# Cross attention of a decoder layer: five steps of the score loop take other places

## The chip, the cores and the metric

One core of a Trainium2 chip runs the kernel. The metric is the device time of one launch in microseconds (us); lower is better. TensorE appears as PE (its weight loads as PEld), VectorE as DVE, ScalarE as ACT, GpSimd as POOL, SyncE as SP.

## What is computed

A decoder layer on x of 8 x 128 x 256: a gated delta-rule attention with 16 key heads, a cross attention, and a mixture of 8 experts with a shared one. The change is in the cross attention:

```python
q = jnp.einsum('oc,bct->bot', Wq, target) + bq[None, :, None]
k = jnp.einsum('oc,bcs->bos', Wk, source) + bk[None, :, None]
v = jnp.einsum('oc,bcs->bos', Wv, source) + bv[None, :, None]
q = q.reshape(b, HEADS, HEAD_DIM, t)          # 8, 16, 8, 256
dot = jnp.einsum('bhdt,bhds->bhts', q, k) / math.sqrt(HEAD_DIM)
dot = mask * dot - (1.0 - mask) * NEG
amap = jax.nn.softmax(dot, axis=-1) * mask
out = jnp.einsum('bhts,bhds->bhdt', amap, v)
```

with 8 batches, 16 heads of width 8, 256 targets (channels of x) and 256 sources (channels of the context).

## The kernel before

Every engine has its own program, written out by hand, and they meet at semaphores: `wait_ge` holds everything behind it on its engine, since each queue is worked in order. Up to 700 us of the span runs the delta-rule attention, from 855 us the experts. Between them lies the loop of the cross attention.

The loop counts n from 0. A unit is two heads of one batch; there are `UNITS` = 64, four for each h (half the heads of a batch, 16 values of h). Four iterations, 4k to 4k+3, are one cycle. Every score is computed twice. First `top_scores(n)` (PE, L1622) puts scores with targets on the partitions into a pair of PSUM banks, and `maxima(n)` (DVE, L1164) takes the largest of each row. When the four units of h are through, POOL's `split_max` writes the negated maxima as two fp16 parts (L595 to L599), `turn_max(h)` (PE, L1632) transposes them into the bank `misc`, and `q_full_(h)` (DVE, L1152) adds them into the stacked queries `qst`. Then, `LAG` = 9 iterations behind, `energies(n-9)` (PE, L1643) computes the scores with sources on the partitions, the maximum already taken off, `weights(n-9)` (ACT, L822) is their exponential into `et`, and three iterations later `values` (PE, L1657) multiplies by v, with ones beside it for the sums. After eight `values` a batch is complete: `gather(b)` (ACT, L829) copies sums and products out of the bank `avb`, SP moves rows with 16 small DMAs (L411), `inverse(b)` (ACT, L834 and L837) inverts the sums, and POOL's `weigh` and `add_x` finish the batch.

Queries come the same way, ahead of use: `q_proj(h, 0)` at the end of iteration 4k+3 and `q_proj(h, 1)` at the end of 4k (PE, L1609 and L1610) fill `misc`, `q_split` (ACT, L816) makes the fp16 part `qh`, and `q_stack_` (DVE, L1157) writes `qst`, first used by `top_scores` of the next cycle. `misc` is shared: `turn_max` waits for the `q_stack_` before it, and `q_proj(h, 0)` for `q_full_`.

Scores use three pairs of banks in turn (`pair_of`): maxima and energies alternate. `energies` in iteration n so takes the pair that `maxima(n-1)` reads, and `top_scores(n)` the pair that the weights of iteration n-2 read. Both matmuls use 32 rows of the array for each head: iteration n's scores lie on row groups 2(n%2) and 2(n%2)+1, its energies, nine units behind, on the other two. `values` uses all 128 rows.

Of the kernel before, what the change touches and what calls it, by code (L numbers as in the profile page):

```python
# [21 lines left out]
B, T, H = 8, 128, 256  # L22
# [18 lines left out]
UNITS = B * 8  # L41
LAG = 9
# [61 lines left out]
def need(eng, sem, value):  # L104

    if isinstance(value, int) and value <= 0:
        return
    eng.wait_ge(sem, value)
# [13 lines left out]
def build(nc, d, out):  # L122
    with ExitStack() as whole:
# [218 lines left out]
        def pair_of(kind, n):  # L342
            if kind == "exp" and n >= UNITS - LAG:
                return pairs[2 - (n - UNITS + LAG) % 2]
            return pairs[place[kind, n] % 3]
# [298 lines left out]
        def norm_act(act, n, bs):  # L644

            act.wait_ge(aggr_done, (0, B, B, 2 * B, 2 * B)[n] + bs.stop)
            if n == 0:
                act.wait_ge(eps_set, 1)
            nc.scalar.activation(lnv[:, bs], mv[:, bs, 1], ACT.Ln, bias=epsc[:, 0:1]).then_inc(lnvar_done, 1)
            act.wait_ge(lnvar_done, n + 1)  # L650
            nc.scalar.activation(rstd[:, bs], lnv[:, bs], ACT.Exp, scale=-0.5).then_inc(rstd_done, 1)

        @block.scalar
        def _(act):
# [158 lines left out]
            def q_split(h):  # L813
                act.wait_ge(q_psum, h + 1)
                need(act, q_stack, h - 1)
                s.activation(qh[:, h % 2], misc, ACT.Copy).then_inc(q_high, 1)  # L816

            def weights(n):
                gq, rp = n // 2, n % 2
                act.wait_ge(e_psum, n + 1)  # L820
                need(act, o_psum, gq - 3)
                s.activation(et[:, gq % 4, 2 * rp:2 * rp + 2].rearrange("p r a t -> p (r a t)"), pair_of("exp", n).rearrange("p r n -> p (r n)"),  # L822
                             ACT.Exp, scale=XD ** -0.5).then_inc(e_done, 1)

            def gather(b):
                act.wait_ge(o_psum, 4 * b + 4)
                need(act, den_moved[b % 2], 128 * (b // 2))
                need(act, num_moved[b % 2], 128 * (b // 2))
                s.activation(avs[:, b % 2], avb, ACT.Copy).then_inc(av_sb, 1)  # L829

            def inverse(b):
                act.wait_ge(den_moved[b % 2], 128 * (b // 2 + 1))
                need(act, den_exp, b)
                s.activation(lden[:], moved[:, b % 2, 1], ACT.Ln).then_inc(den_ln, 1)  # L834
                act.wait_ge(den_ln, b + 1)
                need(act, den_masked, b - 1)
                s.activation(rden[:, b % 2], lden[:], ACT.Exp, scale=-1.0).then_inc(den_exp, 1)  # L837

            def route_exp(gr):
                act.wait_ge(lg_max[gr], 2)  # L840
                s.activation(expl[:, gr], logit[:, gr], ACT.Exp).then_inc(lg_exp[gr], 1)
# [15 lines left out]
            q_split(0)  # L857
            q_split(1)
            for n in range(UNITS + LAG):
                if n >= LAG:  # L860
                    weights(n - LAG)
                m = n - LAG - 10
                if m >= 0 and m % 8 == 0:
                    gather(m // 8)
                if m >= 4 and m % 8 == 4:
                    inverse(m // 8)
                if n >= 4 and n % 4 == 0 and n // 4 + 1 < 2 * B:
                    q_split(n // 4 + 1)
                if n == 56:
                    norm_act(act, 3, slice(0, NB))  # L870
                if n == UNITS + LAG - 3:
                    route_exp(0)
# [20 lines left out]
        def moments(dve, n, bs):  # L893
            v = nc.vector
            done = (0, B, B, 2 * B, 2 * B)[n]
            for b in range(bs.start, bs.stop):
                if n == 0:
                    dve.wait_ge(x_loaded[b], 16)
                elif n < 3:
                    dve.wait_ge(added, (STEPS - 2 + n) * 2)  # L900
                else:
                    dve.wait_ge(xdone, b + 1)
                v.bn_stats(stats[:, b], x1[:, b]).then_inc(stats_done, 1)
            for b in range(bs.start, bs.stop):
                dve.wait_ge(stats_done, done + b + 1)
                v.bn_aggr(mv[:, b], stats[:, b]).then_inc(aggr_done, 1)

        def normalize(dve, n, bs):
            v = nc.vector
            dve.wait_ge(rstd_done, n + 1)  # L910
            for b in range(bs.start, bs.stop):
                v.tensor_scalar(xn[:, b], x1[:, b], mv[:, b, 0:1], rstd[:, b:b + 1], ALU.subtract, ALU.mult).then_inc(xn_done, 1)

        @block.vector
        def _(dve):
# [233 lines left out]
            def q_full_(h):  # L1149
                dve.wait_ge(row_psum, h + 1)  # L1150
                q = qst[:, h % 4].rearrange("p g n -> p (g n)")
                v.tensor_tensor(q, q, misc.bitcast(F16)[:, 0:2 * H], ALU.add).then_inc(q_full, 1)  # L1152

            def q_stack_(h):
                dve.wait_ge(q_high, h + 1)
                need(dve, e_psum, 4 * (h - 3))
                v.scalar_tensor_tensor(out=qst[:, h % 4].rearrange("p g n -> p (g n)"), in0=qh[:, h % 2], scalar=stackcol[:, 0:1], in1=misc,  # L1157
                                       op0=ALU.mult, op1=ALU.add).then_inc(q_stack, 1)

            def maxima(n):  # L1160
                h, g2, rp = n // 4, n // 2 % 2, n % 2
                dve.wait_ge(max_psum, n + 1)
                need(dve, max_scaled, h - 1)
                v.tensor_reduce(mx[:, h % 2, g2, 2 * rp:2 * rp + 2].rearrange("p r a -> p (r a)"),  # L1164
                                pair_of("max", n).rearrange("p r (a s) -> p (r a) s", a=2), AX.X, ALU.max).then_inc(max_done, 1)
# [52 lines left out]
            for n in range(UNITS + LAG + 12):  # L1218
                if n < UNITS:
                    maxima(n)  # L1220
                if n % 4 == 1 and 1 <= n // 4 <= 2 * B:
                    q_full_(n // 4 - 1)
                if n >= 4 and n % 4 == 0 and n // 4 + 1 < 2 * B:
                    q_stack_(n // 4 + 1)
                if n == 54:
                    moments(dve, 3, slice(0, NB))
                if n == 58:
                    normalize(dve, 3, slice(0, NB))
# [52 lines left out]
        def _(pe):  # L1281
# [314 lines left out]
            def pair_free(kind, n):  # L1596
                user = freed(kind, n)
                if user is not None:
                    pe.wait_ge(max_done if user[0] == "max" else e_done, user[1] + 1)
# [35 lines left out]
            def energies(n):  # L1635
                h, g2, rp = n // 4, n // 2 % 2, n % 2
                b, gq = h // 2, h % 2 * 2 + g2
                pe.wait_ge(q_full, h + 1)
                pair_free("exp", n)
                for st in range(2):  # L1640
                    for rr in range(2):
                        ps = slice(32 * (2 * rp + rr), 32 * (2 * rp + rr) + 32)
                        mm = t.matmul(pair_of("exp", n)[:, rr, st * H:(st + 1) * H], kst[ps, b, gq, st * P:(st + 1) * P], qst[ps, h % 4, g2, :], start=True, stop=True)  # L1643
                mm.then_inc(e_psum, 1)
# [51 lines left out]
            for n in range(UNITS + LAG + 3):  # L1696
                if n == UNITS + 2:
                    turn_features(0)
                if n == UNITS + 4:
                    router(0)  # L1700
                if n == UNITS + LAG + 1:
                    turn_comb(0)
                if n < UNITS:
                    top_scores(n)
                if LAG <= n < UNITS + LAG:
                    energies(n - LAG)
                m = n - LAG - 3
                if m >= 0:
                    values(m // 2, m % 2)
                if n % 4 == 1 and 1 <= n // 4 <= 2 * B:  # L1710
                    turn_max(n // 4 - 1)
                if n % 4 == 3 and n // 4 + 2 < 2 * B:
                    q_proj(n // 4 + 2, 0)
                if n >= 4 and n % 4 == 0 and n // 4 + 1 < 2 * B:
                    q_proj(n // 4 + 1, 1)
# [143 lines left out]
```

## Time and profile before

| | |
|---|---|
| median of 3 timed runs | 934.5 us (929.63 to 935.48) |
| profiled execution, timed | 927.55 us |
| its span | 925.7 us |
| busy: PE, DVE, ACT, POOL | 825.7, 721.8, 615.1, 536.7 us |
| mean granted clock of TensorE | 0.933 |

A line of the page's timeline gives the start and length in us, the engine (SPq is SyncE's DMA queue), the line of the kernel, the operation, what it writes and reads with shapes, how many were merged, and in brackets how long the engine sat idle before and what ended that. In a list of stretches, PEclk is the granted clock as a share of 2.4 GHz: it is 1.0 (2.4 GHz) or 0.5 (1.2 GHz), and a value between is a mean over both. Matmuls overlap each other, so the distance of two starts tells what a group costs, its length also how long the last of it takes to run out.

### The profile page before, as it was taken

The page shows a single profiled execution, that of the slowest core. Times are in us where ns is not written, and L with a number is a line of the kernel's source. Part 1 is how long each engine was busy: PE and PEld are TensorE (multiplying, and loading weights), DVE is VectorE, ACT ScalarE, POOL GpSimd, SP SyncE. Part 2 cuts the span into 40 slices and gives each one's busy share as a digit, 9 for nine tenths or more (in the row PEclk, how much of TensorE's full clock was granted, in tenths as well). Part 3 has the DMA queues.
Part 4 walks back from the last instruction along what each step waited for, and adds up shares of the span by engine and source line. Part 5 has one row for each costly group of instructions (what it writes and reads, how often), then busy time and mean ns, then how long its engine had stood idle before and what let it go on. Part 6 is the DMA issues. An engine that isn't in the chain of part 4 may idle for free. (4 is left out here: it accounts for less than half of the span.)

```text
span 925.7 us, 21913 instructions
## 1 busy us (share of the span) xinstructions
PE 825.7 (89%) x7371; PEld 529.6 (57%) x7408; DVE 721.8 (78%) x1227; ACT 615.1 (66%) x1020; POOL 536.7 (58%) x689
## 2 busy tenths in 40 slices
PE   3677999999999999999999999996896888899897
PEld 1445776677677766776677766775553332323353
DVE  8689888888888888887888888884537676774746
ACT  3666887887788877887888878873331465667522
POOL 6466769669697696886966968577103232321300
PEclk9798999999999999999999999998966597967999
DMA  5302011010110100101101010000001510000000
GB/s 160 93 1 80 2 36 36 1 36 0 34 34 0 34 27 7 34 0 34 34 0 34 2 32 11 2 2 1 1 1 27 86 23 18 18 14 24 12 23 24
DMA packets 34416, 23.98 MB, mean 26 GB/s; under 512 B 5062, under 2 KB 33414, under 8 KB 34235
## 3 DMA queue, kind: packets, MB, share of 16 engines
q1 hardware_dynamic: 31643, 19.00, 7.2%
q0 software_dynamic: 2720, 4.29, 2.3%
q8 instruction: 32, 0.52, 0.2%
q14 instruction: 21, 0.17, 0.1%
HBM read 22.68 MB, written 1.05 MB: 26 GB/s over the span
## 5 line engine op out<-in xcount | busy, mean ns | idle before, releaser
L1025 DVE SCALAR_TENSOR_TENSOR y<-psum,cwh,y 128x508 f32<-128x508 f32 (+2 forms) x384 | 281.4, 740 | 21.8 <-ACT y L701 15.8
L491 POOL TENSOR_TENSOR ct<-lm,levels 128x256 f16<-128x256 f32 x224 | 151.7, 699 | 12.0 <-DVE lm L1048 12.0
L477 POOL TENSOR_TENSOR sql<-sq,sqh 128x1024 f16<-128x1024 f32 x32 | 68.4, 2137 | 117.8 <-ACT sq L748 117.8
L701 ACT ACTIVATE y<-psum,cwh 128x512 f32<-128x512 f32 x128 | 99.3, 776 | 47.0 <-PE psum L1312 47.0
L1341 PE MATMUL psum<-wo,vt 128*128 128x256 f32 x512 | 126.0, 389 | 1.2 <-DVE y L1025 1.0
L1341 PEld LDWEIGHTS psum<-wo,vt 128*128 128x128 f32 x512 | 92.3, 190 | 11.9 <-DVE y L1025 2.0
L1164 DVE TENSOR_REDUCE mx<-psum 128x4 f32<-128x1024 f32 x64 | 77.4, 1219 | 20.4 <-PE psum L1622 20.1
L822 ACT ACTIVATE et<-psum 128x1024 f32<-128x1024 f32 x64 | 65.0, 1021 | 41.6 <-PE psum L1643 41.6
L1005 DVE TENSOR_TENSOR ux<-ux,psum 128x512 f16<-128x512 f16 x64 | 43.9, 687 | 55.2 <-PE psum L1425 54.0
L1312 PE MATMUL psum<-xth,whi 128*128 128x512 f16 x256 | 79.3, 392 | 7.0 <-DVE xtl L924 2.7
L1312 PE MATMUL psum<-xtl,whi 128*128 128x512 f16 x256 | 78.4, 389 | 0.0
L1312 PE MATMUL psum<-xth,wlo 128*128 128x512 f16 x256 | 78.4, 389 | 0.0
L993 DVE TENSOR_TENSOR ux<-ux,psum 128x512 f16<-128x512 f16 x96 | 65.0, 677 | 5.7 <-PE psum L1425 5.6
L509 POOL TENSOR_TENSOR lml<-lm,lmh 128x1024 f16<-128x1024 f32 x32 | 68.3, 2135 | 0.0
L1415 PE MATMUL psum<-ux,ct 128*128 128x64 f16 x768 | 55.3, 195 | 14.1 <-DVE ux L1005 7.3
L1422 PEld LDWEIGHTS psum<-t1z,ux 128*128 128x128 f16 x768 | 47.2, 98 | 33.1 <-ACT t1z L683 2.8
L1507 PE MATMUL psum<-zz,pt 128*128 128x256 f32 x256 | 60.5, 379 | 0.0
L499 POOL TENSOR_TENSOR lmh<-lm,zero 128x1024 f16<-128x1024 f32 x32 | 60.5, 1889 | 0.0
L1422 PE MATMUL psum<-t1z,ux 128*128 128x64 f16 x768 | 54.5, 194 | 3.7 <-ACT t1z L688 2.2
L1415 PEld LDWEIGHTS psum<-ux,ct 128*128 128x128 f16 x768 | 37.5, 98 | 32.6 <-DVE ux L1005 12.7
L1507 PEld LDWEIGHTS psum<-zz,pt 128*128 128x128 f32 x256 | 48.5, 190 | 6.5
L595 POOL TENSOR_SCALAR mxs<-mx 128x16 f32<-128x16 f32 x16 | 4.0, 252 | 82.8 <-DVE mx L1164 82.8
(213 smaller groups left out, 2010.2 us busy)
## 6 DMA issues: line engine op xcount, KB each, us to landing
wraw<-in_L_attn_Wv SPq DMA_DIRECT2D x32, 128.0 KB, 2.7
wo<-in_L_attn_Wo SPq DMA_DIRECT2D x16, 256.0 KB, 2.8
wraw<-in_L_attn_Wk SPq DMA_DIRECT2D x16, 128.0 KB, 2.5
wraw<-in_L_attn_Wq SPq DMA_DIRECT2D x16, 128.0 KB, 2.8
moved<-avs SPq DMA_DIRECT2D x128, 16.0 KB, 1.8
x<-in_x SPq DMA_DIRECT2D x8, 128.0 KB, 4.4
maskrow<-in_mask_row POOLq DMA_DIRECT2D x1, 1024.0 KB, 5.3
xt<-in_ctx SPq DMA_DIRECT2D x1, 1024.0 KB, 6.4
```

The lines of the kernel that those rows point to most:

```text
L477: g.tensor_tensor(lo, f, hi, ALU.subtract).then_inc(sq_split, 1)
L491: g.tensor_tensor(dst, src, pick.unsqueeze(1).to_broadcast([P, NB, T // (2 * m), m]), ALU.mult).then_inc(masked[l], 1)
L509: g.tensor_tensor(lo, f, hi, ALU.subtract).then_inc(lm_low, 1)
L701: s.activation(y[:, n], ubank[n % 2].rearrange("p (j t) -> p j t", j=NB), ACT.Identity, scale=cwh[:, (a.c // 2) % 2, n, TAPS - 1:TAPS], bi ...
L822: s.activation(et[:, gq % 4, 2 * rp:2 * rp + 2].rearrange("p r a t -> p (r a t)"), pair_of("exp", n).rearrange("p r n -> p (r n)"), ACT.Ex ...
L1025: v.scalar_tensor_tensor(out=y[:, n, :, sh:], in0=u[:, :, 0:T - sh], scalar=cwh[:, (a.c // 2) % 2, n, TAPS - 1 - sh:TAPS - sh], in1=y[:, n ...
L1164: v.tensor_reduce(mx[:, h % 2, g2, 2 * rp:2 * rp + 2].rearrange("p r a -> p (r a)"), pair_of("max", n).rearrange("p r (a s) -> p (r a) s", ...
L1312: mm = t.matmul(ubank[n % 2], w_[:, hr, n, ch, :], x_[:, ch, cols], start=(m == 0), stop=(m == len(ops) - 1))
L1341: mm = t.matmul(ubank[n][:, j * H:(j + 1) * H], vt[:, r, vc, (2 * n + j) * T:(2 * n + j + 1) * T], wo[:, hr, vc, :], start=(vc == 0), stop ...
L1415: mm = t.matmul(half(dst[:, j * 64:(j + 1) * 64], m), ct[:, st.c % 2, level, j], first_half(turned(st.c % 2, 1, j), m), start=True, stop=True)
L1422: mm = t.matmul(half(dst[:, 256 + j * 64:256 + (j + 1) * 64], m), turned(st.c % 2, 0, j), first_half(t1z[:, level - 1, j * T:(j + 1) * T], ...
L1507: mm = t.matmul((ctk, cx)[hf][:, jj * H:(jj + 1) * H], pt[:, j], zz[:, d.c % 2, j], start=True, stop=True)
```

## The change

Inside the loop over n, five steps take other places; no instruction changes. On PE, `values` stands ahead of `energies` in each iteration, and `turn_max` at the end of iteration 4k+2 in place of 4k+1. On DVE, `q_stack_` comes behind the maxima of 4k+1 in place of 4k, and `q_full_` behind those of 4k+2 in place of 4k+1. On ACT, `gather` comes ahead of `weights` of the same iteration.

```diff
@@ ACT @@
             for n in range(UNITS + LAG):
-                if n >= LAG:
-                    weights(n - LAG)
                 m = n - LAG - 10
                 if m >= 0 and m % 8 == 0:
                     gather(m // 8)
+                if n >= LAG:
+                    weights(n - LAG)
                 if m >= 4 and m % 8 == 4:
                     inverse(m // 8)
@@ DVE @@
                 if n < UNITS:
                     maxima(n)
-                if n % 4 == 1 and 1 <= n // 4 <= 2 * B:
+                if n % 4 == 2 and 1 <= n // 4 <= 2 * B:
                     q_full_(n // 4 - 1)
-                if n >= 4 and n % 4 == 0 and n // 4 + 1 < 2 * B:
+                if n >= 4 and n % 4 == 1 and n // 4 + 1 < 2 * B:
                     q_stack_(n // 4 + 1)
@@ PE @@
                 if n < UNITS:
                     top_scores(n)
-                if LAG <= n < UNITS + LAG:
-                    energies(n - LAG)
                 m = n - LAG - 3
                 if m >= 0:
                     values(m // 2, m % 2)
-                if n % 4 == 1 and 1 <= n // 4 <= 2 * B:
+                if LAG <= n < UNITS + LAG:
+                    energies(n - LAG)
+                if n % 4 == 2 and 1 <= n // 4 <= 2 * B:
                     turn_max(n // 4 - 1)
```

## Rows read from the trace of the kernel before

**Rows 1.** Timeline of DVE: start, length, engine, line, operation, tiles, [idle before, releaser]

```profile
739.71 0.75 DVE L1157 SCALAR_TENSOR_TENSOR qst<-qh,stackcol,psum 128x512 f16<-128x512 f16 x1 [0.81 <-ACT qh L816]
...
764.14 0.75 DVE L1157 SCALAR_TENSOR_TENSOR qst<-qh,stackcol,psum 128x512 f16<-128x512 f16 x1 [0.94 <-ACT qh L816]
...
774.31 0.75 DVE L1157 SCALAR_TENSOR_TENSOR qst<-qh,stackcol,psum 128x512 f16<-128x512 f16 x1 [1.88 <-ACT qh L816]
...
825.65 0.75 DVE L1157 SCALAR_TENSOR_TENSOR qst<-qh,stackcol,psum 128x512 f16<-128x512 f16 x1 [1.88 <-ACT qh L816]
```

**Rows 2.** Stretches of the span: busy time and instructions of each engine, clock, DMA

```profile
739.71:825.65 85.94, 74.28 (x744) 26.85 (x740) 59.40 (x68) 51.92 (x66) 23.54 (x68) 0.84 0.10 21
748.00:766.00 18.00, 14.38 (x173) 5.53 (x166) 13.44 (x15) 11.81 (x15) 5.08 (x14) 1.00 0.07 18
768.00:781.00 13.00, 12.87 (x95) 4.18 (x93) 6.51 (x7) 6.89 (x9) 3.94 (x10) 0.50 0.05 13
```

**Rows 3.** Timeline, all engines, one cycle at full clock

```profile
783.48 0.75 DVE L1157 SCALAR_TENSOR_TENSOR qst<-qh,stackcol,psum 128x512 f16<-128x512 f16 x1 [0.81 <-ACT qh L816]
...
785.51 0.39 PE L1643 MATMUL psum<-qst,kst 32*128 32x256 f16 x4 [0.47 <-DVE mx L1164]
...
785.83 0.64 PE L1657 MATMUL psum<-et,vz 128*32 128x256 f32 x8
...
786.40 0.39 PE L1622 MATMUL psum<-kst,qst 32*128 32x256 f16 x4
...
786.97 0.39 PE L1643 MATMUL psum<-qst,kst 32*128 32x256 f16 x4 [0.18 <-DVE mx L1164]
...
787.86 0.70 PE L1609 MATMUL psum<-xm,wqs 128*128 128x256 f32 x2
...
788.50 0.28 PE L1610 MATMUL psum<-mask,bias 4*128 4x256 f16 x1
...
788.92 0.64 PE L1657 MATMUL psum<-et,vz 128*32 128x256 f32 x8
789.04 1.22 DVE L1164 TENSOR_REDUCE mx<-psum 128x4 f32<-128x1024 f32 x1 [0.98 <-PE psum L1622]
...
790.13 0.39 PE L1622 MATMUL psum<-kst,qst 32*128 32x256 f16 x4
...
790.41 0.39 PE L1643 MATMUL psum<-qst,kst 32*128 32x256 f16 x4
...
791.07 0.75 DVE L1157 SCALAR_TENSOR_TENSOR qst<-qh,stackcol,psum 128x512 f16<-128x512 f16 x1 [0.81 <-ACT qh L816]
...
791.92 0.38 PE L1632 MATMUL psum<-ident,mrow 128*128 128x128 f16 x4 [0.55 <-issue]
```

**Rows 4.** Timeline of PE, where the clock falls and at half clock

```profile
766.49 0.64 PE L1657 MATMUL psum<-et,vz 128*32 128x256 f32 x8
...
767.63 0.61 PE L1643 MATMUL psum<-qst,kst 32*128 32x256 f16 x4 [0.18 <-DVE mx L1164]
768.17 1.08 PE L1657 MATMUL psum<-et,vz 128*32 128x256 f32 x8
769.18 1.22 PE L1609 MATMUL psum<-xm,wqs 128*128 128x256 f32 x2
770.34 0.39 PE L1610 MATMUL psum<-mask,bias 4*128 4x256 f16 x1
...
777.88 0.39 PE L1622 MATMUL psum<-kst,qst 32*128 32x256 f16 x2
...
778.43 1.08 PE L1657 MATMUL psum<-et,vz 128*32 128x256 f32 x8
```

**Rows 5.** Timeline of ACT, a copy of the sums and the inverse after it

```profile
830.94 0.60 ACT L829 ACTIVATE avs<-psum 128x512 f32<-128x512 f32 x1
...
838.92 0.42 ACT L834 ACTIVATE lden<-moved 128x256 f32<-128x256 f32 x1 [0.22 <-DMA moved<-avs]
```

**Rows 6.** Timeline of DVE, the layer norm's statistics inside the loop

```profile
818.75 1.39 DVE L903 BATCH_NORM_STATS2 stats<-x 128x6 f32<-128x256 f32 x4
```

## The prediction

> **What bounds the kernel now.** The profiled execution spans 925.7 us (927.55 us timed; the three timed runs have their median at 934.5). I read the DVE timeline first, for the period of a cycle, then the list of stretches for clock and busy shares, then one cycle on PE and DVE line by line at each clock. The change touches only the attention loop over n (64 score units, four to a head pair h; I call four units a cycle). Ten cycles, from the sixth q_stack_ to the sixteenth, take 825.65 - 739.71 = 85.94 us [rows 1], in which the granted clock averages 0.84: since the two levels are 1.2 and 2.4 GHz (0.5 and 1.0), 32% of the time is at the lower one [rows 2].
>
> At full clock a cycle takes 791.07 - 783.48 = 7.59 us [rows 3], and no engine is full: PE 14.38, DVE 13.44, ACT 11.81 us busy of 18 [rows 2]. So the order of waits sets the time, not an engine. PE's cycle, from starts [rows 3]: scores for the maxima (T) 790.41 - 790.13 = 0.28, energies (E) 785.83 - 785.51 = 0.32, values (V) 786.40 - 785.83 = 0.57, one half of q_proj 788.50 - 787.86 = 0.64. The turning of the maxima is put at T's 0.28 to E's 0.32; I take 0.32. Once a cycle, behind q_proj, T and E are issued into each other and cost 0.42 together (788.50 to 788.92) where apart they cost 0.60. Sum: 4 x 1.17 + 2 x 0.63 + 0.32 - 0.18 = 6.08 us. The other 1.5 us are three waits, which the idle brackets show as 0.55, 0.47 and 0.18 [rows 3] (the rest of each is the run-out of the matmul ahead):
>
> - turn_max, at the end of iteration 4k+1, stands until q_stack_ (791.07, 0.75 long) is done at 791.82, and starts at 791.92. Behind it in PE's queue stand the next T and everything after.
> - That q_stack_ stood on DVE ahead of the maxima of 4k+1, whose T was done since 790.5; so those maxima came 1.2 us late, and the E that takes their PSUM pair waits for them. V stands behind E in program order, though it wants only weights of two iterations before.
> - DVE then starves for 0.98 us (the reduction at 789.04) because the next T is behind the V and the q_proj that were held up.
>
> At half clock PE is 100% busy and the period is 774.31 - 764.14 = 10.17 us [rows 1]. Apart, E costs 768.17 - 767.63 = 0.54, V 769.18 - 768.17 = 1.01, half a q_proj 770.34 - 769.18 = 1.16; T and E inside each other cost 0.55 together (777.88 to 778.43) [rows 4].
>
> **The change, part by part.** No instruction is added or removed; five positions move.
>
> 1. DVE: q_stack_ from behind the maxima of 4k to behind those of 4k+1. The 0.81 us in which DVE waits for ACT's qh [rows 3] is filled with a reduction of 1.22. Its users are T of 4k+4, three iterations on, and turn_max, which moves too. I value this together with 2.
> 2. PE: turn_max from 4k+1 to 4k+2, and DVE's q_full_ with it. The first E that needs it is in 4k+9: four iterations of slack become three, free. The POOL splits end earlier than either place. What remains of the wait: walking a cycle from E(4k) at 0: q_proj to 0.95; T(4k+1) done at 1.3; its maxima 1.4 to 2.6; q_stack_ to 3.4; meanwhile PE does V, E, T, V, E to 3.3; turn_max waits 0.2, ends 3.8; T, V to 4.7; E(4k+3) follows maxima(4k+2), which end at 4.5; q_proj to 5.6 behind q_full_ (4.9); T, V, and E(4k+4) at 6.5. So 0.62 of wait becomes 0.2.
> 3. PE: V ahead of E. The two waits of E on maxima (0.58 and 0.29 with run-out) lie under V's 0.57: about zero. The price: T and E no longer stand side by side, so the 0.18 of overlap goes at full clock, once a cycle. E is now beside the next T, but n-9 and n+1 have the same parity, so both are on the same two row groups and share nothing.
> 4. ACT: gather ahead of the weights. PE now issues the last V of a batch before that iteration's E, so the copy (0.6) is due first; the next V comes 0.3 + 0.63 + 0.28 later, after it is done. The weights behind it slip 0.4; T of two iterations on is 2 us away. Free. Without this move the next V would stand behind the weights too, which are most of ACT's 5.0 busy us a cycle (11.81 of 18 us [rows 2]), so behind about 1 us more.
>
> New PE sum at full clock: 6.08 + 0.18 + 0.2 of wait = 6.5 us; I take 6.55 for transitions that the trace doesn't show (E directly before T). Ends for it: 6.26 (no wait left) and 7.59 (each wait only moves). DVE, 4 x 1.22 + 0.75 + 0.41 = 6.0, and ACT, 5.0, stay below. So PE is the bound at full clock, nearly without gaps.
> At half clock PE is full before and after, and loses the overlap: 4 x (0.54 + 1.01 + 0.54) + 2.3 + 0.55 = 11.2 us against 10.17: 1 us worse.
>
> "TensorE: Matmul & The Clock Gate" of the Trainium skill (Part 3, row/col tiling) speaks against part 3: matmuls on different 32-row groups run at the same time. By that rule each of the four T and E pairs of a cycle could save 256 columns at 2.4 GHz, an estimate of 0.11 to 0.21 us, and breaking all four up would cost up to 0.85 a cycle, 8.5 over ten. The trace agrees on the size (0.18) but shows it at full clock once a cycle only, since elsewhere E stands waiting.
>
> **The clock.** At 766.5 a V takes 0.64 us, at 767.6 an E already takes 0.61 where it took 0.39, at 768.2 the V takes 1.08 [rows 4]: the clock fell from 2.4 to 1.2 GHz within iterations 4k+2 and 4k+3, where PE has both E waits, and there I found all its four falls inside the ten cycles. It then stayed low though PE was busy 12.87 of 13 us, against 14.38 of 18 at full clock, so busy time alone doesn't bring it back [rows 2]. The new cycle has no such thin place, so I expect most of the 32% to go, but leave 7 of the remaining 67 us at half clock: each us there costs 1 - 6.55/11.2 = 0.42, so 3 us.
>
> **Sum.** Ten cycles: 85.94 - 65.5 = 20.4 gained. Less 1.8 for the layer norm on DVE inside these cycles (4 statistics in 1.39 us [rows 6], the normalisation taken as long, less DVE's slack): hidden beside a half-clock PE now, and more than fits between 6.0 and 6.55 then. Less 3 for the clock. First cycles, at half clock in any case: 0.5 lost (lost overlap 0.55 to 0.65 in some four iterations, against turn_max's gap). End of the loop: the last turning is one iteration later, so the router's input is too: V + E, 1 us. 20.4 - 1.8 - 3 - 0.5 - 1 = 14. Profiled time 927.55 - 14 = 913.5; the profiled run is 7 below the median, so for the median 934.5 - 14 = 920.5; I say 920.
>
> **Rivals.**
> (a) The waits go, but the clock stays low for 32% of the time. Per cycle 1/(0.68/6.55 + 0.32/11.2) = 7.55: gain 85.94 - 75.5 - 3.3 = 7: 927. For it: PE was full and still at 1.2 GHz for 13 us [rows 2]. Against: the thin place goes.
> (b) The wait only moves: gather to inverse is one cycle plus some 0.7. ACT's inverse came 838.92 - (830.94 + 0.60) = 7.4 us after a copy and waited 0.22 for DMA [rows 5]. At 6.55 + 0.7 that is just late, and the weights are queued behind it. Up to 1 us in every second cycle, 5 in all, plus a turn_max wait of 0.6 as before, 4: 929.
> (c) Other side: half clock holds. If more than half of the loop is at 1.2 GHz the gain is gone (10 cycles in 82: 8.2 = 1/((1-s)/6.55 + s/11.2) gives s = 0.5); if all of it is, ten cycles take 112 us, 26 more: about 960; at 70%, 945. For it: the change lowers the work per us exactly there. Against: the clock rose each time before, in a fuller PE.
> (d) It does nothing because the next thing in the chain is as late (cycle 7.4 to 7.6, lost overlap at half clock): 934.
>
> **Chances.** Forecast 0.5, (a) 0.2, (b) 0.1, (c) 0.1, (d) 0.1. About 1%, 9 us, is what a measurement of this kernel can tell. Faster than 925: the forecast, nearly half of (a), a little of (b): 0.62. Within 1%: 0.26. Slower: 0.12. Range: from 908 (6.3 us a cycle, clock full: 21 gained, and runs 5 below their median) to 933, which takes in (a) and (b).
>
> **What would show it.** Right: q_stack_ starts 6.4 to 6.7 us apart at full clock, no DVE wait on qh, E without an idle bracket, clock 1.0 in most of the loop, PE over 95% busy. Part 2 wrong: turn_max idle over 0.5. Part 3 wrong: idle before V instead, on weights. (b): ACT lden idle on DMA in the middle of the loop. Nothing outside the loop should move by over 1 us.

## The result: slower by 4%, with the clock low for the whole loop

The changed kernel takes 969.83 us (median of 4 runs, 968.35 to 973.54) against 933.08 us (929.63 to 935.48): ratio 1.040, 95% interval 1.035 to 1.045. I had forecast 920, between 908 and 933. What came is rival (c), which I had priced at "about 960" and given one chance in ten. The mean granted clock over the span was 0.873 to 0.879 in all four runs, so it is not the chance of one profile.

The page of the changed kernel: its span, and the granted clock in 40 equal slices (tenths; 9 is 90% or more).

```profile
span 966.5 us, 21913 instructions
...
PEclk9798999999999999999999999989655555555999
```

From the slice that starts at 701 us to the one that ends at 894 the clock is at 5 tenths. The ten cycles of the prediction, from the sixth to the sixteenth `q_stack_` on the DVE timeline (start, length, engine, line, operation), and the same stretch in the list of stretches (length; busy us of PE, PEld, DVE, ACT, POOL; clock; DMA share; GB/s):

```profile
745.53 0.74 DVE L1157 SCALAR_TENSOR_TENSOR qst<-qh,stackcol,psum 128x512 f16<-128x512 f16 x1
...
858.60 0.74 DVE L1157 SCALAR_TENSOR_TENSOR qst<-qh,stackcol,psum 128x512 f16<-128x512 f16 x1
```

```profile
745.53:858.60 113.07, 113.07 (x744) 35.24 (x742) 61.24 (x70) 53.49 (x67) 24.67 (x69) 0.50 0.05 13
```

They take 858.60 - 745.53 = 113.07 us, 11.31 a cycle, against 85.94 [rows 1]. PE is busy 113.07 of 113.07 us, at a clock of 0.50, where it was busy 74.28 of 85.94 at 0.84 [rows 2]. One part of a cycle, PE's timeline of the changed kernel:

```profile
790.52 0.61 PE L1643 MATMUL psum<-qst,kst 32*128 32x256 f16 x4
790.92 0.63 PE L1622 MATMUL psum<-kst,qst 32*128 32x256 f16 x4
791.48 1.08 PE L1657 MATMUL psum<-et,vz 128*32 128x256 f32 x8
792.50 0.60 PE L1643 MATMUL psum<-qst,kst 32*128 32x256 f16 x4
793.03 0.61 PE L1632 MATMUL psum<-ident,mrow 128*128 128x128 f16 x4
793.57 0.61 PE L1622 MATMUL psum<-kst,qst 32*128 32x256 f16 x4
794.11 1.08 PE L1657 MATMUL psum<-et,vz 128*32 128x256 f32 x8
795.13 0.61 PE L1643 MATMUL psum<-qst,kst 32*128 32x256 f16 x4
```

There is no idle bracket left: the wait of `turn_max` and both waits of the energies are gone [rows 3], as the change means it. But every group has its half-clock price: V 1.02 us (792.50 - 791.48), E 0.53 (793.03 - 792.50), the turning 0.54, T 0.54. T and E of one iteration stand apart. Only once a cycle, where an E stands directly ahead of the next T, do the two share a little: 0.40 from start to start (790.92 - 790.52), where E apart costs 0.53.

Where the 40.8 us of the two profiled spans (966.5 - 925.7) lie: 27.1 in these ten cycles; 5.8 ahead of them, of which 1.9 (706.10 - 704.19 at the first `q_stack_`) come from code ahead of the loop that did not change; 7.9 behind them, in the rest of the loop and its end. From the fourth to the fifth `q_stack_` it took 8.96 us (9.15 before); from the fifth to the sixth 11.31, where the kernel before got its clock back and took 8.69.

### The profile page after: what moved, and what is told of

It reads as the page before. It is cut to its first block and busy times, and to the rows that moved or that the text cites. A ratio compares the mean times of both kernels' runs of the same rounds, so it can differ in the third digit from the quotient of the medians.

```text
span 966.5 us, 21913 instructions
## 1 busy us (share of the span) xinstructions
PE 878.7 (91%) x7371; PEld 542.4 (56%) x7408; DVE 722.5 (75%) x1227; ACT 617.3 (64%) x1020; POOL 538.7 (56%) x689
## 3 DMA queue, kind: packets, MB, share of 16 engines
HBM read 22.68 MB, written 1.05 MB: 25 GB/s over the span
## 5 line engine op out<-in xcount | busy, mean ns | idle before, releaser
L1657 PE MATMUL psum<-et,vz 128*32 128x256 f32 x512 | 68.8, 632 | 0.0
```

The lines of the kernel that those rows point to most:

```text
L1657: mm = t.matmul(avb[ps, gq // 2 * H:(gq // 2 + 1) * H], vz[:, b % 2, st, r, gq], et[:, gn % 4, r, st], start=(gq == 0 and st == 0), stop=( ...
```

## Experiments

Theory: the order T, V, E takes the overlap of T and E away; at 1.2 GHz PE then does less work per us although it is always busy, and the clock stays low. Rival: the later turning and stacking do it. Each result names the ratio to the kernel before on the same chip.

### e1_values_first: only values and the copy of the sums move

```diff
 # the kernel before, with the ACT hunk of the change and this on PE
+                    values(m // 2, m % 2)
                 if LAG <= n < UNITS + LAG:
                     energies(n - LAG)
-                m = n - LAG - 3
-                if m >= 0:
-                    values(m // 2, m % 2)
```

> Only values go ahead of energies (and the copy of the sums with them); turning and stacking stay where they were before. Theory 'lost overlap': with T (scores for the maxima) and E (energies) no longer side by side, PE at 1.2 GHz takes about 11 us a cycle and stays there, so this part alone is enough: clock 0.5 for most of the loop and 960 to 975 us. Rival 'turning later': the moved turn and stack steps are what keeps the clock low; then this kernel keeps its clock as before (0.8 or more in the loop) and, with E's waits covered by V, takes 920 to 935 us.

Measured: 966.11 us, ratio 1.037 (1.033 to 1.041). Its ten cycles:

```profile
744.23:857.29 113.06, 113.06 (x748) 35.17 (x740) 60.30 (x68) 53.09 (x66) 24.66 (x69) 0.50 0.05 13
```

113.06 us with PE full at 0.50, the changed kernel's figure to 0.01 us. This part alone makes the loss, but for the 4 us between the two medians.

### e2_turn_later: only turning, q_full_ and q_stack_ move

```diff
 # the kernel before, with the DVE hunk of the change and this on PE
-                if n % 4 == 1 and 1 <= n // 4 <= 2 * B:
+                if n % 4 == 2 and 1 <= n // 4 <= 2 * B:
                     turn_max(n // 4 - 1)
```

> Only turn_max, q_full_ and q_stack_ move; energies stay ahead of values and the copy behind the weights. Lost overlap: T and E stay side by side, the wait of turn_max (0.6 us) goes, a full-clock cycle takes about 7.0 us against 7.6, the clock is at least as high as before: 920 to 932 us. Turning later: clock 0.5 for most of the loop, over 955 us.

Measured: 911.71 us, ratio 0.981 (0.976 to 0.985), faster than both kernels and than I expected. Its ten cycles, and the stretch at full clock among them:

```profile
737.61:808.36 70.75, 64.62 (x740) 24.90 (x740) 58.49 (x69) 51.57 (x68) 23.47 (x68) 0.98 0.15 30
740.00:797.00 57.00, 52.84 (x622) 20.55 (x621) 47.33 (x50) 43.24 (x55) 20.86 (x59) 1.00 0.11 25
```

70.75 us against 85.94, with the clock at 0.98. Part of a cycle on PE:

```profile
757.60 0.39 PE L1622 MATMUL psum<-kst,qst 32*128 32x256 f16 x4
758.36 0.39 PE L1643 MATMUL psum<-qst,kst 32*128 32x256 f16 x4 [0.37 <-DVE mx L1164]
758.68 0.64 PE L1657 MATMUL psum<-et,vz 128*32 128x256 f32 x8
759.25 0.40 PE L1632 MATMUL psum<-ident,mrow 128*128 128x128 f16 x4
759.58 0.39 PE L1622 MATMUL psum<-kst,qst 32*128 32x256 f16 x4
760.15 0.39 PE L1643 MATMUL psum<-qst,kst 32*128 32x256 f16 x4 [0.18 <-DVE mx L1164]
```

`turn_max` (L1632) starts right behind V, so its wait is gone. The two waits of E on the maxima are still there, 0.37 and 0.18. From 737.61 to 799.03 `q_stack_` came nine times more, 6.82 us apart, against 7.59 [rows 3]. So the thin place at which the clock fell before need not vanish for the clock to hold; less of it was enough. The clock also came up earlier: a V takes 1.08 us at 727.11 and 0.64 at 729.71, where the kernel before still has 1.08 at 735.15 and 0.64 from 737.56 on.

### e3_burst: the changed kernel with 24 dense matmuls ahead of the first V

```diff
             for n in range(UNITS + LAG + 3):
+                if n == LAG + 3:
+                    for _ in range(24):
+                        t.matmul(avb[:], kst[:, 0, 0, 0:P], kst[:, 0, 0:2, :].rearrange("p g n -> p (g n)"), start=True, stop=True, skip_group_check=True)
```

The products go to the bank of the values, which starts afresh behind them.

> The changed kernel with 24 extra matmuls of 128x128 by 512 columns before the first V, once (about 10 us at 1.2 GHz, 5 at 2.4); nothing else differs. Theory 'two states': at 2.4 GHz the new cycle is dense enough to hold the clock, it only never gets there. Then the loop runs at 2.4 GHz behind the burst in cycles of 6.5 us, and the time is 925 to 935 us. Rival 'too thin at either clock': the clock falls again within a cycle or two, and the time is 970 to 980 us.

Measured: 919.54 us, ratio 0.990 (0.987 to 0.993): 50 us less than the changed kernel, for 6.6 us of extra work, and below the 925 to 935 I gave. PE's timeline around the burst, then the DVE timeline and the list of stretches for the ten cycles behind it:

```profile
725.02 1.22 PE L1609 MATMUL psum<-xm,wqs 128*128 128x256 f32 x2
...
726.49 6.71 PE L1699 MATMUL psum<-kst 128*128 128x512 f16 x24
733.13 0.39 PE L1622 MATMUL psum<-kst,qst 32*128 32x256 f16 x4
733.46 0.64 PE L1657 MATMUL psum<-et,vz 128*32 128x256 f32 x8
734.03 0.39 PE L1643 MATMUL psum<-qst,kst 32*128 32x256 f16 x4
```

```profile
743.09 0.74 DVE L1157 SCALAR_TENSOR_TENSOR qst<-qh,stackcol,psum 128x512 f16<-128x512 f16 x1
...
749.62 0.74 DVE L1157 SCALAR_TENSOR_TENSOR qst<-qh,stackcol,psum 128x512 f16<-128x512 f16 x1
...
802.02 0.74 DVE L1157 SCALAR_TENSOR_TENSOR qst<-qh,stackcol,psum 128x512 f16<-128x512 f16 x1
...
809.60 0.74 DVE L1157 SCALAR_TENSOR_TENSOR qst<-qh,stackcol,psum 128x512 f16<-128x512 f16 x1
```

```profile
743.09:809.60 66.51, 65.27 (x744) 25.41 (x742) 58.57 (x69) 52.05 (x68) 23.14 (x67) 1.00 0.08 22
```

The q_proj ahead of the burst has instructions of 1.22 us, the V behind it 0.64: the clock rose within the burst. Then it is 1.00 through all ten cycles, PE is busy 65.27 of 66.51 us, and a cycle takes 6.53 us (749.62 - 743.09). The same loop body takes 11.31 or 6.53 us, and kept the clock that it had, low or high, for these ten cycles. Not further, though. The layer norm on DVE makes two E wait for their maxima. The first wait, 0.98 us at 807.07, left the clock up; behind the second, just after the ten cycles, it is gone at once and stays away for some 13 us:

```profile
814.38 0.43 PE L1643 MATMUL psum<-qst,kst 32*128 32x256 f16 x4 [1.22 <-DVE mx L1164]
814.60 0.64 PE L1622 MATMUL psum<-kst,qst 32*128 32x256 f16 x4
```

### e5_burst_thin: the same burst on 32 rows and 32 columns

```diff
-                        t.matmul(avb[:], kst[:, 0, 0, 0:P], kst[:, 0, 0:2, :]...
+                        t.matmul(avb[0:32], kst[0:32, 0, 0, 0:32], kst[0:32, 0, 0:2, :]...
```

> The changed kernel with the same 24 extra matmuls of 512 columns at the same place, but each on 32 rows and 32 columns of the array in place of 128 and 128: PE is as long busy. If it is how much of the array works that brings the clock up, the clock stays at 1.2 GHz behind them and the time is that of the changed kernel plus about 10 us, 970 to 980 us. If PE's busy time, or the pause that DVE and ACT get, brings it up, the loop runs as behind the dense burst: 915 to 930 us.

Measured: 978.02 us, ratio 1.052 (1.048 to 1.056). PE's timeline:

```profile
729.41 1.22 PE L1609 MATMUL psum<-xm,wqs 128*128 128x256 f32 x2
...
730.88 10.42 PE L1699 MATMUL psum<-kst 32*32 32x512 f16 x24
741.23 0.61 PE L1622 MATMUL psum<-kst,qst 32*128 32x256 f16 x4
741.77 1.08 PE L1657 MATMUL psum<-et,vz 128*32 128x256 f32 x8
```

24 matmuls of as many columns, 10.4 us without a gap, and behind them the V still takes 1.08 us. The ten cycles took 113.07 us again. So neither PE's busy time nor the pause for the other engines brings the clock up; the dense burst differs from this one in the part of the array that works (and in the rows and columns of memory that go with it).

### e6_before_burst: the dense burst in the kernel before

The same three lines, in the kernel before.

> The kernel before with the dense burst of 24 matmuls (128x128 by 512 columns) ahead of its first V. If the new order is what holds the clock at 2.4 GHz once it is there, the kernel before still loses it behind its waits, several times, in cycles of 7.6 us, and takes 925 to 935 us, as without the burst. If any order holds it after such a start, its loop stays at 2.4 GHz and it takes 915 to 922 us.

Measured: 937.69 us, ratio 1.010 (1.007 to 1.013), a little above the 925 to 935 I gave. Its ten cycles:

```profile
747.85:834.84 86.99, 75.56 (x740) 27.20 (x740) 59.41 (x68) 51.83 (x66) 23.25 (x68) 0.82 0.06 17
```

86.99 us at 0.82, against 85.94 at 0.84 [rows 2]: the kernel before loses its clock again and again whatever it starts with, the changed one keeps a high clock for the ten cycles. So the dense loop of the change does hold the clock once it has it, as long as nothing makes it wait; what it did not do by itself is come up.

### e8_e2_lag8: the old order, the overlap taken away

If T and E must lie on different row groups to share the array, 8 units of distance in place of 9 take that away with the order T, E, V untouched.

```diff
 # on e2_turn_later
-LAG = 9
+LAG = 8
-            return pairs[place[kind, n] % 3]
+            return pairs[(place[kind, n] + 2) % 3]
```

The second line only renames the bank pairs, so that the last units end in those that the code behind expects.

> The fast half of the change (turning and stacking later, energies still ahead of values) with energies 8 units behind in place of 9. The order T, E, V stays, but T and E of an iteration now lie on the same two row groups. Theory 'lost overlap': a cycle at 1.2 GHz takes about 11 us although the order is the old one, the clock comes up late or not at all, and the time is 935 to 965 us against 912. If the order T, V, E itself were the cause, and not the row groups, it stays at 905 to 918 us.

Measured: 961.63 us, ratio 1.035 (1.031 to 1.039); e2 had 911.71 us and 0.981. A T, an E and a V of it at half clock, then its ten cycles:

```profile
777.13 0.61 PE L1622 MATMUL psum<-kst,qst 32*128 32x256 f16 x4
777.53 0.64 PE L1643 MATMUL psum<-qst,kst 32*128 32x256 f16 x4
778.10 1.08 PE L1657 MATMUL psum<-et,vz 128*32 128x256 f32 x8
779.11 0.61 PE L1632 MATMUL psum<-ident,mrow 128*128 128x128 f16 x4
```

```profile
744.02:853.35 109.33, 108.19 (x744) 39.79 (x740) 61.15 (x70) 53.55 (x68) 24.30 (x69) 0.52 0.05 13
```

T and E together take 778.10 - 777.13 = 0.97 us; with different row groups they took 0.55 [rows 4]. A cycle takes 10.93 us in the mean (10.97 where it is all at half clock), the clock is 0.52: it came up for some 3 us near the end, and fell again where an E had stood 1.14 us behind DVE's maxima (848.87). PE is busy 108.19 of 109.33 us, so no wait that the shorter lag might bring makes the cycle long. The number 9 was what let scores and energies share the array, and 50 us hang on 9 in place of 8. This is the cleanest evidence that the lost overlap is the cause and not the order as such; and it is not the shorter lag either, since in e4, below, the same two lines take 47 us away.

### e4_lag8: the changed order, part of the overlap given back

The same two lines on the changed kernel: there E of one iteration and T of the next, which stand side by side, come to lie on different row groups.

> The changed kernel with energies 8 units behind the maxima in place of 9 (and the three bank pairs renamed so that the last units end where the code behind expects them). E of an iteration and T of the next then lie on different row groups. Lost overlap: they are issued into each other, a cycle at 1.2 GHz takes about 9.1 us in place of 11.3, at 2.4 GHz 5.6 to 6.2 (DVE's own sum is 6.0), and the time is 895 to 925 us. If the overlap has nothing to do with it: 965 to 970 us.

Measured: 922.84 us, ratio 0.990 (0.987 to 0.994), 47 less than the changed kernel. PE around one such pair at half clock, and two stretches, one ahead of the rise of the clock and one behind:

```profile
753.49 1.08 PE L1657 MATMUL psum<-et,vz 128*32 128x256 f32 x8
754.51 0.40 PE L1643 MATMUL psum<-qst,kst 32*128 32x256 f16 x2
754.52 0.40 PE L1622 MATMUL psum<-kst,qst 32*128 32x256 f16 x2
754.70 0.42 PE L1643 MATMUL psum<-qst,kst 32*128 32x256 f16 x2
754.71 0.42 PE L1622 MATMUL psum<-kst,qst 32*128 32x256 f16 x2
755.06 1.08 PE L1657 MATMUL psum<-et,vz 128*32 128x256 f32 x8
```

```profile
733.00:757.00 24.00, 24.00 (x172) 7.14 (x164) 13.60 (x15) 11.19 (x13) 2.89 (x11) 0.50 0.49 85
758.00:808.00 50.00, 48.49 (x572) 18.31 (x572) 42.84 (x45) 38.47 (x50) 19.30 (x55) 1.00 0.08 19
```

E and T are issued into each other (754.51 to 755.06, 0.55 us for both), but only once a cycle, since q_proj or the turning stands between them in the other three; so a half-clock cycle takes 10.9 us (754.75 - 743.85 on the DVE timeline), not the 9.1 I expected. The clock was down over 25 us longer than in e3 and then came up by itself, between the two stretches.

### e9_lag8_burst, e10_e2_spread, e11_e9_spread: towards a faster version

e9 is e4 with the dense burst. In e10 (on e2) and e11 (on e9) the layer norm that DVE does inside the loop goes one batch at a time:

```diff
-                if n == 54:
-                    moments(dve, 3, slice(0, NB))
-                if n == 58:
-                    normalize(dve, 3, slice(0, NB))
+                if 51 <= n < 51 + NB:
+                    moments(dve, 3, slice(n - 51, n - 50))
+                if 58 <= n < 58 + NB:
+                    normalize(dve, 3, slice(n - 58, n - 57))
```

> The changed kernel with energies 8 units behind (overlap between E and the next T) and the dense burst ahead of the first V. Its loop holds 2.4 GHz from the fourth cycle on in cycles of 6.5 us, three cycles of 10.9 us at 1.2 GHz less than without the burst: 922.8 less 13 plus 5 for the burst, 910 to 917 us, no worse than the fast half of the change alone. If the clock is lost at the end of the loop as early as behind the other burst, 918 to 923 us.

> The fast half of the change (turning and stacking later, energies ahead of values), and the layer norm's statistics and normalisations taken one at a time in eight iterations of the loop in place of four at once in two. In the fast half alone E stood 1.0 us behind the four statistics at 803 and the clock was 1.2 GHz for 3.4 us from there. If such a gap is what lets the clock fall, it stays at 2.4 GHz through those cycles and the time is 906 to 911 us against 911.7. If the fall comes of the loop's end itself, no change: 909 to 915 us.

> The changed kernel with energies 8 units behind and the dense burst, and the layer norm spread in the same way. There E stood 0.98 and 1.49 us behind the layer norm at 807 and 814, ahead of the fall at 816. If those gaps let it fall, the clock holds to the end of the maxima and the time is 902 to 909 us against 912.2; if not, 910 to 914 us.

Measured: e9 912.18 us, ratio 0.981 (0.977 to 0.985); e10 910.06, 0.977 (0.973 to 0.981); e11 911.46, 0.978 (0.974 to 0.982). e9 came as expected (910 to 917). In its profile E waits twice for maxima that stand behind DVE's layer norm, and then the clock falls (E at 816.12 still takes 0.39, T at 816.59 already 0.61); in e11 no E waits longer than 0.52:

```profile
807.69 0.39 PE L1643 MATMUL psum<-qst,kst 32*128 32x256 f16 x4 [0.98 <-DVE mx L1164]
...
814.99 0.39 PE L1643 MATMUL psum<-qst,kst 32*128 32x256 f16 x4 [1.49 <-DVE mx L1164]
...
816.12 0.39 PE L1643 MATMUL psum<-qst,kst 32*128 32x256 f16 x4
816.59 0.61 PE L1622 MATMUL psum<-kst,qst 32*128 32x256 f16 x4
```

```profile
807.64 0.39 PE L1643 MATMUL psum<-qst,kst 32*128 32x256 f16 x4 [0.45 <-DVE mx L1164]
...
815.98 0.37 PE L1643 MATMUL psum<-qst,kst 32*128 32x256 f16 x3 [0.52 <-DVE mx L1164]
```

In e11 the clock stayed up through the last cycles, and so it did in e10, where it is 1.00 from 736 to 824 us; e2 had lost it behind waits of 1.01 and 1.47 us. That fits the waits as what lets it fall. But the medians of e9 and e11 differ by 0.7 us, inside their runs, and those of e2 and e10 by 1.7, also inside those of e2; e10's 910.06 lies in both ranges of its expectation, and e11's 911.46 in the one for no help. So whether the spreading saves time at all isn't settled. All three, and e2, are faster than both kernels by a margin clear of the runs; e2 is the smallest edit, e10 the lowest median.

## Why the prediction was wrong, point by point

- **Durations.** Half clock, predicted 11.2 us a cycle: 11.31. Full clock, 6.55: 6.53 (e3). The first held to 0.1 us, each part within that. The second held in part by luck: it has 0.2 us of wait of `turn_max`, and in e3 there is no such bracket; but T ahead of V costs 0.31 to 0.42 (744.56 - 744.24, 746.52 - 746.10), where I had 0.28 four times. The 10.17 us of before was read over an interval whose first 3.5 us were still at full clock; a whole cycle at half clock, from V to V, is 778.43 - 768.17 = 10.26 [rows 4].
- **Parts 1 and 2 (stack and turn later).** Right in mechanism and too low in size: the wait of `turn_max` went, DVE no longer waits for qh in the ten cycles, and a cycle at full clock lost 0.77 us (7.59 to 6.82) where I had put 0.42. With the clock that held, that is worth about 18 us on its own (e2).
- **Part 3 (values ahead of energies).** The waits lie under V, as said. The price was put at 0.18 us a cycle at full clock and 1 us at half clock. The second is right (1.1); no run shows the first by itself. That E and the next T share nothing was not quite so: 0.22 us from start to start in e3 (749.16 - 748.94) against 0.32 apart, 0.40 against 0.53 at half clock. What I did with the price is where the forecast failed.
- **Part 4 (copy ahead of the weights).** Free: in e3's ten cycles the copies wait 0.3 us at most for PE, the inverse at most 0.9 us for its DMAs. That is the sign I had named for rival (b), twice in ten cycles (0.22 and 0.88), but it cost next to nothing: the cycle that holds the longer one took 6.68 us in place of 6.53.
- **The clock: the failing step.** I wrote "The new cycle has no such thin place, so I expect most of the 32% to go". That asks only what makes the clock fall. But the loop begins at 1.2 GHz, in both kernels (0.50 in the stretches below, before first, changed second), and I had read that myself for the first cycles ("at half clock in any case"). The question was whether the new loop, at 1.2 GHz, brings it up. In the same text stood the hint: PE was busy 12.87 of 13 us at 0.50 [rows 2], so PE's busy time does not, and the change lowers the work per us in just that state: the same work takes 11.2 us in place of 10.17. I set against rival (c) that "the clock rose each time before, in a fuller PE"; the PE of before was not fuller in time but in array, by the overlap. The chance of 0.1 was far too low, and a little half clock ("7 of the remaining 67 us") was no likely case for this order: e3 shows its ten cycles at 1.00, the changed kernel at 0.50.

```profile
708.00:736.00 28.00, 22.79 (x155) 8.28 (x147) 21.80 (x23) 9.00 (x11) 6.90 (x18) 0.50 0.25 45
...
708.00:736.00 28.00, 23.09 (x137) 8.78 (x138) 20.68 (x22) 7.40 (x9) 7.90 (x23) 0.50 0.23 43
```

- **The rule of the Trainium skill.** I had used "TensorE: Matmul & The Clock Gate" of the Trainium skill (Part 3) for the overlap, priced the loss at up to 0.85 us a cycle by it and 0.18 by the rows, and left out what the overlap does for the clock. (0.85 is four times 0.21, which is 512 columns and not the 256 I wrote.) At half clock the trace of before has T and E inside each other in three of four iterations (at 770.34, 773.25 and 777.88), so there far more than 0.18 was to lose: 1.1 us a cycle (11.31 - 10.17). The table "Why this matters for your kernels" on the same page of the Trainium skill puts a full clock down to keeping TensorE busy without a break. Here the measurement decides otherwise: 113.07 of 113.07 us busy, at 0.50 (busy as the profile counts it, which models where a matmul ends).
- **End of the loop.** 1 us was forecast for the router behind the later turning; PE waits 0.88 us there for the features (at 881.08). The other 7 of the 7.9 us behind the ten cycles I put down to the clock, which is 0.50 there for most of the way; that is a difference, not a measurement.
- **Layer norm on DVE.** 1.8 was forecast; in e3 the cycle that holds the statistics takes 809.60 - 802.02 = 7.58 us against 6.53, so 1.05 for that one. I had put the normalisation inside the ten cycles too; in e3 it lies behind them, where E waits 1.22 us and the clock falls (814.38), a price I had not set.

**Open.** What exactly lifts the clock isn't settled. The dense burst does and the thin one doesn't, so the working part of the array counts and busy time doesn't. But e4, at 10.9 us a cycle, came up by itself some 30 us behind its first V, and e8, at 10.97, only after nearly 120: a cycle's mean rate alone does not decide, and where in the cycle the dense places stand was not tried. Nor is it settled which waits make it fall: in e3 one of 0.98 us did not, one of 1.22 did.

## What to carry to other kernels

When a loop runs near the point where the clock falls, ask two questions: does it keep the clock, and does it get there from below. Sum PE's cycle at 1.2 GHz as carefully as at 2.4, and distrust an edit that makes that sum longer, even where it removes every idle gap. Two matmul groups on different row groups next to each other can be worth more than their time, as they were here; before moving one away, look whether something else (here the parity of a lag) can keep them together.

## What the runs showed of the hardware

- One loop body held either clock: 66.51 us for ten cycles at 1.00 (e3), 113.07 at 0.50 (the changed kernel), though PE had no gap in the second. Behind 24 matmuls of 128x128 by 512 columns (6.6 us) it held the high one, behind 24 of 32x32 by 512 (10.4 us) it stayed low.
- Eight matmuls of 32 rows by 256 columns took 0.55 us at 1.2 GHz when the two groups of four lay on different rows and stood side by side, 0.97 when they lay on the same rows.
- The kernel before, given the same burst, lost the clock again (0.82 over ten cycles), so the good start helped only the loop that had no waits at full clock; and that one lost it too, behind a wait of 1.22 us (e3 at 814.38).
